# Four transformer layers in one kernel: the exponentials of the quantised attentions per head on ScalarE, with maximum, scale and row sums in the same instruction

## The reference, cut to what matters

```python
def _fq(x, delta, zp, n_bits):
    xi = _round_ste(x / delta) + zp
    xq = jnp.clip(xi, 0.0, 2.0 ** n_bits - 1.0)
    return (xq - zp) * delta

def _attn(x, ctx, wq, wk, wv, wo, bo, dq, dk, dv, dw):
    ...
    sim = jnp.einsum('bhid,bhjd->bhij', _fq(q, dq, 128.0, 8), _fq(k, dk, 128.0, 8)) * SCALE
    attn = jax.nn.softmax(sim, axis=-1)
    out = jnp.einsum('bhij,bhjd->bhid', _fq(attn, dw, 0.0, 8), _fq(v, dv, 128.0, 8))
```

## Time and profile before

| | |
|---|---|
| Median of 3 runs | 2164.98 us (2163.7 to 2165.68) |
| The profiled execution's own time | 2164.18 us |
| Its span | 2162.5 us |
| Share of the span: TensorE, weight loads, VectorE, ScalarE, GpSimd | 84%, 63%, 64%, 44%, 46% |
| Chain that ended last, by engine | TensorE 51%, VectorE 17%, issue 5%, ScalarE 5%, GpSimd 4% |
| Granted TensorE clock, mean over the span | 0.914 |

### The profile page before, as it was taken

How to read it: one execution, slowest core, us unless ns; L and a number is a source line. 1 busy time by engine, 2 the same in 40 slices (tenths; PEclk the granted TensorE clock), 3 DMA queues, 4 the chain that set the end, 5 groups by cost and what they waited for, 6 DMA issues and landing times.

```text
span 2162.5 us, 33926 instructions
## 1 busy us (share of the span) xinstructions
PE 1823.1 (84%) x12417; PEld 1356.3 (63%) x12417; DVE 1390.1 (64%) x2348; ACT 940.9 (44%) x2238; POOL 992.8 (46%) x1233
## 2 busy tenths in 40 slices
PE   4766666687887888887899899999999999999997
PEld 4655555555665665665676676666666676676766
DVE  5877778878568658658558565584755736546372
ACT  1111111233333333333457555565555656656563
POOL 4566666555335336336425343453544424333340
PEclk8888888877888887887999999999999999999999
DMA  7200000000110000000000200000000000000000
GB/s 213 87 6 5 5 5 6 10 1 6 34 50 6 6 1 1 6 6 1 6 6 6 84 1 6 6 7 6 1 7 6 6 6 1 26 6 1 11 2 10
DMA packets 31355, 35.87 MB, mean 17 GB/s; under 512 B 3196, under 2 KB 30040, under 8 KB 30808
## 3 DMA queue, kind: packets, MB, share of 16 engines
q1 hardware_dynamic: 31192, 33.70, 5.0%
HBM read 31.60 MB, written 2.10 MB: 16 GB/s over the span
## 4 chain that ended last, share of the span: by engine, by line
PE 51%; DVE 17%; issue 5%; ACT 5%; POOL 4%; DVEq 0%; POOLq 0%; ACTq 0%
PE ps L526 31%; PE ps L713 5%; PE ps L703 5%; PE ps L747 4%; ACT work L879 3%; DVE work L1065 2%; PE ps L538 2%; DVE rowmax L1071 2%; DVE xn L925 2%; DVE rowmax L1069 2%; PE ps L728 2%; DVE rowsum L1077 1%; ACT work L868 1%; DVE O L1104 1%; POOL work L1189 1%
## 5 line engine op out<-in xcount | busy, mean ns | idle before, releaser
L526 PE MATMUL ps<-hT,w_slot 128*128 128x256 f32 x1856 | 449.8, 396 | 18.8 <-ACT hT L794 18.4
L526 PEld LDWEIGHTS ps<-hT,w_slot 128*128 128x128 f32 x1856 | 357.1, 197 | 81.5 <-ACT hT L794 20.4
L1189 POOL TENSOR_TENSOR work<-KT,own_head 128x512 f32<-128x512 f32 x256 | 261.1, 1046 | 247.0 <-ACT KT L806 199.7
L713 PEld LDWEIGHTS ps<-ident,work 128*128 128x128 f32 x1536 | 201.1, 154 | 206.4 <-issue 82.7
L713 PE MATMUL ps<-ident,work 128*128 128x128 f32 x1536 | 265.6, 302 | 54.6 <-POOL work L1265 35.4
L879 ACT ACTIVATE work<-work,rowmax 128x128 f32<-128x128 f32 x768 | 244.9, 391 | 145.6 <-DVE rowmax L1069 144.2
L703 PE MATMUL ps<-work,QT 128*128 128x512 f32 x512 | 267.9, 610 | 14.6 <-POOL work L1189 9.3
L1265 POOL TENSOR_SCALAR work<-work,winv 128x128 f32<-128x128 f32 x512 | 183.1, 378 | 202.8 <-DVE winv L1090 202.1
L1104 DVE RECIPROCAL O<-ps 128x128 f32<-128x128 f32 x128 | 122.1, 954 | 221.9 <-PE ps L747 221.8
L526 PE MATMUL ps<-w_slot,hid 128*128 128x256 f32 x1024 | 227.6, 381 | 0.9 <-ACT hid L839 0.9
L526 PEld LDWEIGHTS ps<-w_slot,hid 128*128 128x128 f32 x1024 | 193.1, 191 | 26.5 <-ACT hid L839 1.3
(11 more groups left out here) (120 smaller groups left out, 3094.2 us busy)
## 6 DMA issues: line engine op xcount, KB each, us to landing
ctx_in<-in_ctx SPq DMA_DIRECT2D x32, 256.0 KB, 2.7
w_slot<-in_L_xattn_W SPq DMA_DIRECT2D x2, 1024.0 KB, 6.1
w_slot<-in_L_xattn_ff_w SPq DMA_DIRECT2D x1, 2048.0 KB, 11.4
w_slot<-in_L_xattn_ffn_w SPq DMA_DIRECT2D x2, 1024.0 KB, 8.7
w_slot<-in_L_xattn_w SPq DMA_DIRECT2D x2, 1024.0 KB, 9.1
out<-x_all SPq DMA_DIRECT2D x8, 256.0 KB, 2.1
x_all<-in_x SPq DMA_DIRECT2D x1, 1536.0 KB, 11.4
pad<-in_mask_Bx1x1xS_fk SPq DMA_DIRECT2D x1, 1024.0 KB, 6.9
```

What stands on the lines that cost most here:

```text
L526: mm = pe.matmul(dst, lhsT(k), rhs(k), start=(k == 0), stop=(k == chunks - 1))
L713: mm = pe.transpose(bank(2 + u % 2)[:, tok(h)], prob[u % (NP if quant else NPF)][:, tok(h)], ident[:, :])
L1189: pool.tensor_tensor(KB[u % NK].rearrange("p (h k) -> p h k", h=HU), keys, own_head[:, e:HC:2].unsqueeze(2).broadcast_to([P, HU, S]), ALU. ...
```

## The change

For quantised attentions alone, ScalarE's exponential becomes four instructions, one per head, that read the scores in PSUM. Each takes the score scale as `scale`, the negated and scaled maximum as `bias`, and writes the row sum of its head to `rowsums` through the accumulator output. VectorE takes the maximum negated, scales these 128x4 values, and neither subtracts nor sums. The scores of unit u wait for `exp_ready` of unit u-2, since the exponentials are now the last to read the bank, and the inverses wait for `exp_ready` of both units of their pair.

```diff
--- before.py
+++ after.py
@@ -307,7 +307,7 @@
 
         once = """keep_loaded keep_ready more_tables vrows_loaded rows_loaded small_loaded x_first x_rest stored waits_passed live_step
             ident_zeroed ident_ready own_set own_half own_ready consts_ready vcols_ps tables_ready
-            KB_ready scores_ps masked max_ready shift_ready exp_ready sums_ready inv_ready winv_ready rounded
+            KB_ready scores_ps masked max_ready shift_ready exp_ready inv_ready winv_ready rounded
             PT_ps PT_ready o_ps oinv_ready o_ready quarter_out V_zeroed
             A_low A_high E_low_ps E_high E_max E_shift E_exp E_sum E_inv E_ready B_low B_high O_high""".split()
         s = {n: sem(n) for n in once}
@@ -691,9 +691,6 @@
 
                     if u >= 2 and "mask" in arg:
                         pe.wait_ge(s["masked"], U * masked_phase(layer, g, mix, st) + u - 1)
-                    elif u >= 2 and quant:
-
-                        pe.wait_ge(s["shift_ready"], U * ap + u - 1)
                     else:
                         pe.wait_ge(s["exp_ready"], U * ap + u - 1)
                     if quant:
@@ -870,8 +867,11 @@
 
                         act.wait_ge(s["shift_ready"], U * ap + i + 1)
                         if quant:
-                            act.activation(prob[i % NP], prob[i % NP], ACT.Exp, scale=score_scale[:, arg["quant"]:arg["quant"] + 1])\
-                                .then_inc(s["exp_ready"], 1)
+                            for h in range(HU):
+                                at = i * HU + h
+                                ex = act.activation(prob[i % NP][:, tok(h)], bank(i % 2)[:, tok(h)], ACT.Exp, bias=shifts[:, at:at + 1],
+                                                    scale=score_scale[:, arg["quant"]:arg["quant"] + 1], accum_out=rowsums[:, at:at + 1])
+                            ex.then_inc(s["exp_ready"], 1)
                         else:
                             src = prob[i % NPF] if "mask" in arg else bank(i % 2)
                             for h in range(HU):
@@ -1068,20 +1068,15 @@
                     if not quant:
                         dve.tensor_reduce(shift_u, sc, AX.X, ALU.max, negate=True).then_inc(s["shift_ready"], 1)
                         return
-                    dve.tensor_reduce(shift_u, sc, AX.X, ALU.max).then_inc(s["max_ready"], 1)
+                    dve.tensor_reduce(shift_u, sc, AX.X, ALU.max, negate=True).then_inc(s["max_ready"], 1)
                     dve.wait_ge(s["max_ready"], U * qp + u + 1)
-                    dve.tensor_tensor(pr, sc, shift_u.unsqueeze(2).broadcast_to([P, HU, S]), ALU.subtract).then_inc(s["shift_ready"], 1)
-
-                def sums(u):
-                    dve.wait_ge(s["exp_ready"], U * ap + u + 1)
-                    dve.tensor_reduce(rowsums[:, u * HU:(u + 1) * HU], prob[u % NP].rearrange("p (h k) -> p h k", h=HU), AX.X, ALU.add)\
-                        .then_inc(s["sums_ready"], 1)
+                    dve.tensor_scalar(shift_u, shift_u, score_scale[:, arg["quant"]:arg["quant"] + 1], None, ALU.mult).then_inc(s["shift_ready"], 1)
 
                 def inverses(pair):
 
                     dw = 4 * arg["quant"] + 3
                     both = slice(pair * 2 * HU, (pair + 1) * 2 * HU)
-                    dve.wait_ge(s["sums_ready"], U * qp + 2 * pair + 2)
+                    dve.wait_ge(s["exp_ready"], U * ap + 2 * pair + 2)
                     dve.reciprocal(rowinv[:, pair % 2, 0:2 * HU], rowsums[:, both]).then_inc(s["inv_ready"], 1)
                     dve.wait_ge(s["inv_ready"], U // 2 * qp + pair + 1)
                     if pair >= 2:
@@ -1108,8 +1103,6 @@
                 def step(i):
                     if i < U:
                         shift(i)
-                    if quant and 0 <= i - SUM_LAG < U:
-                        sums(i - SUM_LAG)
                     if quant and 0 <= i - SUM_LAG < U and (i - SUM_LAG) % 2:
                         inverses((i - SUM_LAG) // 2)
```

## The result

The changed kernel takes 2134.45 us (median of four runs, 2132.68 to 2138.63) against 2165.18 us for the kernel before, run beside it: a ratio of 0.9862 (95% interval 0.9845 to 0.9879), some 30 us faster. The forecast of 2171 us and its range from 2138 us are both missed, on the side of rival 1. The profiled execution was the slowest of the four, 2138.63 us with a span of 2136.9 us, so the two profiles are 25.6 us apart.

What follows compares the result with a forecast made beforehand. VectorE was taken to bound each phase's first half and TensorE the second; after the change, ScalarE's queue alone. Short phases -5, long +7, clock +4 made +6 on 2164.2 us, and 0.8 for the median: 2171 us, range 2138 to 2218.

Steps and rivals of the forecast that it cites:

- rival 1: ScalarE's accumulator output is nearly free, 0.07 to 0.13 us per head; 1.64 us per unit, 2127 us; chance 20%.
- the accumulator output: Row sum leaving ScalarE with each exponential: taken at 0.19 us per head, between 0.07 and 0.31.
- one pointer from PSUM: Exponential of one head read from PSUM with one pointer operand on ScalarE: 0.26 us each.
- the second pointer: Second pointer operand of each ScalarE exponential: 0.08 us start to start.
- The queue sum up to the gate: ScalarE's work in a long phase (feed-forward beside its second half) until the first gate: 7.57 + 8E = 24.4 us.
- The three quarters: In rival 1, the share of the earlier eighth scores that stays, in short and long phases: 38 us.
- below 0.15 us per head: Accumulator price under which rival 1 decides, with E (ScalarE's exponentials per unit) under 1.95 us.
- VectorE costed at nothing: VectorE, with about 1 us per unit for the softmax, is no longer the bound; ScalarE's queue alone is the path.
- The short phase's sum, 3.14 + 6E: Eighth scores after the first, in phases with another attention's projections beside their second half: 15.7 us against 16.58.
- Two phases stood for sixteen: Timelines of two phases, one short and one long, used for eight of each kind: -5 and +7 us.
- The clock: A new TensorE hole before the feed-forward's third block can delay the clock's return: +4 us, between nothing and 29.
- VectorE's busy time: Falls by 128 x (0.69 + 0.67 - 0.21) = 147 us without subtractions and sums, with the scaling added.

Runs made afterwards that it cites:

- the first experiment: The changed kernel plus one useless 128x1 ScalarE copy ahead of each of the 512 exponentials: 2168.43 us, ratio 1.0021 against the kernel before.
- the run with the accumulator alone: Changed kernel with VectorE's subtraction put back, exponentials per head from SBUF with accumulator output, no VectorE sum: 2137.27 us, ratio 0.9877 against the kernel before.

## Why the prediction was wrong

**The step that failed** is the accumulator output, taken at 0.19 us per head as "the row nearest to a read that ends in SBUF". It costs 0.093 (0.436 us with it, 0.343 without). That is inside the bounds of 0.07 and 0.31, next to the lower one. I had chosen the fixed cost of an exponential over 128 columns, an instruction with a hundred times the data. The nearer figure was the one behind the lower bound, the fixed part of a short ScalarE instruction less its overlap, and the useless one-column copy of the first experiment moves the heads by the same 0.092. The middle of a range is no reason to take a value.

**The other terms per head** held: one pointer from PSUM 0.26, measured 0.343 - 0.093 = 0.25; the second pointer 0.08, measured 0.093. The Trainium skill's figure of 93 ns for a pointer (ScalarE: Activation LUTs, What ACT_TABLE_LOAD costs) agrees with that, and the 0.294 us that its figures give for an exponential with one pointer, an estimate, agrees with SBUF, 0.385 - 0.093 = 0.29 us in the run with the accumulator alone; from PSUM, as in the earlier trace rows, a head takes 0.04 us less than it says.

**The queue sum up to the gate** held where ScalarE runs without a stop: 26.1 us for 25.9 and 29.0 for 28.8 in the two runs with added copies. The whole time at 0.528 us per head, 2168 for a forecast of 2171, is weaker evidence, since up to 8 us of it are the moved table loads; without them I estimate 2160 to 2168. So ScalarE's queue was rightly put together, and one term in it was mis-sized by 0.1 us, which the kernel multiplies by 512. At the measured price this queue is no longer the whole path.

**The change of bound** was rival 1's, with its direction and nearly its size: 2127 forecast at 1.64 us per unit, 2134 measured at 1.745. The prediction's own arithmetic for that rival comes closer still with the measured price: 16.58 - 13.6 and 17.26 - 14.7 us, three quarters of both, eight times, make 33 us and 2132. The three quarters were a guess, so this is partly luck. The steps between the runs agree with its "below 0.15 us per head" and don't fix the figure. What was wrong is the 20% that it had, and a range that cut off its outer half.

**VectorE costed at nothing** was wrong at this price. The short phase's sum, 3.14 + 6E, gives 13.6 us for E = 1.745, and in the phase of the earlier trace rows 14.54 are measured. The first exponential starts 1.50 us after the first scores, 0.4 earlier than I took; then ScalarE idles 0.8 us in all for late maxima, and TensorE starts the eighth scores 0.6 us after the sixth unit's exponentials are done. ScalarE, VectorE and TensorE in that phase of the changed kernel:

```profile
508.97 0.46 ACT L872 ACTIVATE work<-ps,rowmax,score_scale 128x128 f32<-128x128 f32 x1 [0.38 <-DVE rowmax L1073]
```

```profile
506.72 1.33 DVE L925 TENSOR_SCALAR xn<-x_all,meanvar,rstd 128x256 f32<-128x256 f32 x2 [0.56 <-POOL rstd L1200]
507.98 0.68 DVE L1071 TENSOR_REDUCE rowmax<-ps 128x4 f32<-128x512 f32 x1
```

```profile
508.20 1.09 PE L538 MATMUL ps<-ident,xn 128*128 128x128 f32 x4 [0.24 <-DVE xn L925]
509.22 0.60 PE L698 MATMUL ps<-work,QKb 64*128 64x512 bf16 x1
```

A LayerNorm step that waits for GpSimd stands in front of a maximum on VectorE, and its transposition in front of the next scores on TensorE. While ScalarE's queue is long enough they are hidden; here they are late. That a sum more on VectorE, which is idle for a quarter of these stretches, costs for the same reason is likely and was not traced.

**Two phases stood for sixteen.** How a phase begins and what stands beside its second half are two things. In the changed kernel four of the short phases begin like the long one shown (eighth scores 15.4 to 16.9 us after the first), and four of the long ones like the short one (14.5 to 14.8). Over all sixteen this roughly cancels, phase by phase it does not.

**Why the sum is dear and the subtraction cheap.** Both took 0.6 us of VectorE. The sum waits for the exponentials and stands in front of the next unit's maximum; its time is worth about 14 us and that wait about 10. The subtraction waits for nothing that comes from ScalarE, and it freed the PSUM bank for the next scores. The change gives this up: in this kernel the scores wait for exponentials. That the freed bank accounts for the small worth of the subtraction is argued from the code and was not tried alone.

**The clock**, +4 in the forecast: the stretch has 0.81 before and after, but its cost can be seen in the first halves of the two profiles, where TensorE's same work is busy 180.9 instead of 174.7 us. In the long phase of the earlier trace rows the output projection behind the second scores, before and after:

```profile
584.36 1.99 PE L526 MATMUL ps<-w_slot,OT 128*128 128x256 f32 x8
```

```profile
576.35 3.19 PE L526 MATMUL ps<-w_slot,OT 128*128 128x256 f32 x8
```

The granted clock from the first to the third scores is 1.00 before and 0.76 after. The third scores come 5.15 us after the first instead of 3.96, and ScalarE stands idle for the 0.71 us shown above. How much of this reaches the whole time was not separated; the sixteen output projections together take 40.3 us instead of 37.0.

**VectorE's busy time** fell by 119 us and not 147, since I had added the rows' durations. Start to start the two instructions take 1.21 us; less 0.26 for the scaling this makes 122.

## What to carry to other kernels

When one instruction repeats some hundred times on an engine that is about to become the bound, settle its price before everything else, and take an unknown one from the row with the nearest amount of data, not from the middle of its bounds. A row sum that leaves as a by-product of the exponentials pays twice, by the time that it takes off VectorE (some 14 us here) and by the wait that it takes out of VectorE's queue (some 10), so look at what the instruction waits for and what stands behind it. An instruction added to measure a price can move others: look in its trace for table loads and waits that changed place. A sum of one engine's queue holds only down to the point where the next engine's chain is as long; past it, each further saving brings a fraction.

## What the runs showed of the hardware that was not expected

An accumulator output on ScalarE is a second instruction whose row is 190 ns (the accumulator alone, from SBUF) to 256 ns (one added copy) long in the mean and yet moves the next one by only 93 ns.

In these kernels a table load runs directly ahead of the first instruction that needs it. A copy put in front of the exponentials ran without one, so the load of 1.28 us came to stand behind the copy's wait, in the path, in six phases.

While ScalarE runs back to back, its rows grow longer and their starts do not move: in the long phase above an exponential goes from 0.46 to 0.59 us and the read from 0.19 to 0.34, with 0.343 and 0.093 us from start to start all along, and after an idle stretch of 0.71 us both are short again. Means of such rows, as 482 ns for an exponential, overstate the cost; only the distance of starts gives it.
